# Attention and a gated feed-forward layer on one core: where the row-maximum matmuls stand among the score chunks

## What is computed

```python
def attention(h, ...):                      # h = layernorm(x)
    q, k, v = (proj(W, b) for ...)          # B, 16 heads, 512, 8
    idx = clip(pos[None, :] - pos[:, None], -20, 20) + 20
    attn1 = einsum('bhqd,bhkd->bhqk', q, k)
    attn2 = einsum('bhqd,qkd->bhqk', q, rel_k[idx])
    attn = softmax((attn1 + attn2) / sqrt(8), axis=-1)
    w1 = einsum('bhqk,bhkd->bhqd', attn, v)
    w2 = einsum('bhqk,qkd->bhqd', attn, rel_v[idx])
    return (w1 + w2) @ Wo.T + bo
x = x + attention(layernorm(x))
x = x + ffn(layernorm(x))                   # down(silu(gate) * up)
```

## Time and profile before

| | |
|---|---|
| median of three runs | 1260.71 us (1256.79 to 1262.96) |
| the profiled execution | 1265.17 us, its span 1263.4 us |
| mean granted TensorE clock | 0.991 |
| busy share | TensorE 96%, VectorE 72%, ScalarE 58%, GpSimd 46% |
| attention stage, row maxima | 1024 reductions, 658.5 us of VectorE |
| operand loads and the rest of SyncE's queue | 72.67 MB |

### The profile page before, as it was taken

How to read it: one execution, slowest core, us unless ns; L and a number is a source line. 1 busy time by engine, 2 the same in 40 slices (tenths; PEclk the granted TensorE clock), 3 DMA queues, 4 the chain that set the end, 5 groups by cost and what they waited for, 6 DMA issues and landing times. The chain is left out here.

```text
span 1263.4 us, 60291 instructions
## 1 busy us (share of the span) xinstructions
PE 1207.8 (96%) x27042; PEld 828.2 (66%) x27042; DVE 912.2 (72%) x1747; ACT 735.7 (58%) x1382; POOL 578.1 (46%) x1083
## 2 busy tenths in 40 slices
PE   6988999999999999999999999999999999999998
PEld 4554466767666666666666666676666677666675
DVE  6886877777777767777777777777777776156664
ACT  6885255656666656566666666666666566523322
POOL 5986554444445444443435454444454444022221
PEclk9998999999999989999999999999999999999999
DMA  5776202120203030303021221213030300023221
GB/s 169 228 233 201 54 5 45 34 55 24 63 20 68 12 69 10 70 9 69 22 57 36 52 50 37 57 30 72 20 69 11 70 10 10 12 68 98 77 76 51
DMA packets 101001, 76.52 MB, mean 61 GB/s; under 512 B 12744, under 2 KB 96520, under 8 KB 100744
## 3 DMA queue, kind: packets, MB, share of 16 engines
q1 hardware_dynamic: 100744, 72.67, 22.0%
HBM read 44.86 MB, written 26.21 MB: 56 GB/s over the span
## 5 line engine op out<-in xcount | busy, mean ns | idle before, releaser
L1210 DVE TENSOR_REDUCE b_mx<-b_a 128x1 f32<-128x512 f32 x1024 | 658.5, 685 | 220.5 <-PE b_a L877 218.7
L1155 ACT ACTIVATE b_p<-b_s 128x512 f32<-128x512 f32 x1024 | 569.6, 595 | 366.6 <-PE b_s L936 224.6
L823 POOL TENSOR_TENSOR qd<-q,one 48x512 bf16<-48x512 bf16 x256 | 266.2, 1040 | 453.2 <-PE b_s L936 433.9
L992 PE MATMUL b_pv<-b_p,vg 128*32 128x256 f32 x4096 | 276.3, 383 | 0.0
L936 PE MATMUL b_s<-qd,z 112*128 112x32 bf16 (+1 forms) x6016 | 248.7, 188 | 3.4 <-issue 3.3
L936 PEld LDWEIGHTS b_s<-qd,z 112*128 112x128 bf16 (+1 forms) x6016 | 204.1, 98 | 13.6 <-issue 3.8
L877 PE MATMUL b_a<-k,q 48*128 48x512 bf16 x1024 | 199.8, 386 | 11.3 <-DVE b_mx L1210 3.0
L898 PE MATMUL b_s<-q,k 54*128 54x64 bf16 (+5 forms) x4096 | 186.2, 205 | 8.2 <-DMA q<-b_mt 7.1
L898 PEld LDWEIGHTS b_s<-q,k 54*128 54x128 bf16 (+1 forms) x4096 | 111.4, 95 | 103.0 <-PE b_s L898 29.8
L992 PEld LDWEIGHTS b_pv<-b_p,vg 128*32 128x32 f32 x4096 | 117.4, 109 | 59.8 <-issue 20.3
L945 PE MATMUL b_s<-q,k 118*128 118x64 bf16 x2048 | 104.7, 195 | 2.6 <-issue 2.6
(11 more groups left out here) (146 smaller groups left out, 1263.3 us busy)
## 6 DMA issues: line engine op xcount, KB each, us to landing
x<-in_x SPq DMA_DIRECT2D x24, 256.0 KB, 3.4
scratch_qop<-a_parts SPq DMA_DIRECT2D x16, 384.0 KB, 2.6
scratch_kop<-a_parts SPq DMA_DIRECT2D x16, 384.0 KB, 3.4
k<-scratch_kop SPq DMA_DIRECT2D x32, 192.0 KB
q<-scratch_qop SPq DMA_DIRECT2D x32, 192.0 KB
scratch_v<-a_vr SPq DMA_DIRECT2D x16, 256.0 KB, 3.5
k<-scratch_kop SPq DMA_DIRECT2D x32, 128.0 KB
q<-scratch_qop SPq DMA_DIRECT2D x32, 128.0 KB
```

The costliest lines, as they stand in the source:

```text
L823: nc.gpsimd.tensor_tensor(dst, src, one, ALU.mult).then_inc(s["qd_ready"], 1)
L992: nc.tensor.matmul(PV[V32 * a:V32 * (a + 1), g * PT:(g + 1) * PT], v[:, side, half, t, 2 * a + g, :], PR[pos][:, 4 * a + 2 * half + g, :], ...
L1155: nc.scalar.activation(out, src, ACT.Exp, scale=SCALE).then_inc(s["p_ready"], 1)
L1210: nc.vector.tensor_reduce(MX[unit.v % 2][:, h:h + 1], PA[(HP * n + hp) % NBANK][:, :], AX_X, ALU.max, negate=True).then_inc(s["a_used"], 1)
```

## The change

The diff is given whole. `EXTRA` loses its two entries of pair 1. From pair 1 on `pairs_beside` gives chunks 1 and 9 no row pair and chunks 4 and 12 two; in chunks 2 to 4 and 10 to 12 it counts from one lower, so that the order of row pairs stays unbroken. From pair 1 on they run 16 ahead of the chunks, not 18 as they did from chunk 13 of pair 1 on. The twelve operand loads of an even pair stand one to a chunk in chunks 0 to 11, the value loads in chunk 12.

```diff
-PIECES = ((0, 1), (2,), (3,), (4, 5), (6, 7), (8, 9), (10, 11))
...
-EXTRA = (0, 1, 12, 14, CHUNKS + 4, CHUNKS + 12)
+EXTRA = (0, 1, 12, 14)
...
         n = CHUNKS * pair + c
         first = n + FIRST + sum(e < n for e in EXTRA)
-        return [r for r in range(first, first + 1 + (n in EXTRA)) if r < HH * U]
+        count = 1 + (n in EXTRA)
+        if pair:
+            first -= c in (2, 3, 4, 10, 11, 12)
+            count += (c in (4, 12)) - (c in (1, 9))
+        return [r for r in range(first, first + count) if r < HH * U]
...
                 for c in range(CHUNKS):
-                    if ahead and c < len(PIECES):
+                    if ahead and c < NLOAD:
                         sp.wait_ge(s["s_ready"], PB2 * pair + 2 * c + 1)
-                        load_score_operands(sp, k, d, batch + 1, (batch + 1) % 2, PIECES[c])
-                    if ahead and c == len(PIECES) + 1:
+                        load_score_operands(sp, k, d, batch + 1, (batch + 1) % 2, [c])
+                    if ahead and c == NLOAD:
                         sp.wait_ge(s["s_ready"], PB2 * pair + 2 * c + 1)
                         load_values(sp, k, d, batch + 1, (batch + 1) % 2)
```

## The result

The changed kernel takes 1280.72 us, the median of four runs (1279.23 to 1282.36), against 1261.12 for four runs of the kernel before beside it (1256.79 to 1262.96). The ratio on record is 1.0124, 95% interval 1.0082 to 1.0167. The two medians by themselves give 1.0155; 1.0124 would go with a kernel before of 1265 us, close to its medians in the later sets. So it is slower by 1.2 to 1.6%, clear of noise. Its profiled execution took 1281.19 us, 16.0 more than that of before, with a span of 1278.4, 15.0 more.

What follows compares the result with a forecast made beforehand. TensorE's order and waits were taken to bound the kernel. Terms -26.4 (removed row pairs), +56.0 (doubles), +0.4 (lead) and -14 (loads) gave +16 us, so 1277 us for the median, own range 1268 to 1287, stated range 1266 to 1294.

Steps and rivals of the forecast that it cites:

- The doubles: Second row pairs in chunks 4 and 12, pairs 2 to 30: 0.965 us each, mostly wait, +56.0 us together.
- Rival 4: Second row pair of a double doesn't wait, costing 0.21 us only: 1232 us; chance 0.06.
- The removed row pair: Chunks 1 and 9, pairs 1 to 30: each removal gives 0.44 us of TensorE, -26.4 us together.
- The lead: Row pairs 16 ahead, not 18: +0.4 us for pair 30; minus parts keep about 2.3 us of cover.
- The loads: One load to a chunk in even pairs: -14 us, between 0 and the 21.7 us lost there.
- the guard rows' 8 us: Loads' first term: TensorE's waits for guard rows in even pairs fall, 8 us won, between 6.2 and 9.9.
- The 5 us for "issue" waits: Loads' term for TensorE waits the profile doesn't explain, in loaded pairs, and their clock: 5 us won, bounds 0 and 11.
- The sum: Whole kernel: +16 us on the profiled execution, 1277 us for the median, slower by 1.3%; chance 0.68.
- No relief (1): Waits in the even pairs stay or others take their place: 1260.7 + 30 = 1291 us; chance 0.12.
- Late operands (2): Last q load lands after the next pair's chunk 0 wants it, 1.7 us in 14 pairs: about 1307 us; chance 0.08.
- No clock loss (3): Denies the rival that waits in every pair bring TensorE's clock down: +52 us, 1329 us; chance 0.03.
- That the parts merely cancel (5): Change does less than it says, or some cover is accidental, and parts cancel: near 1261 us; chance 0.03.

Runs made afterwards that it cites:

- one double: Changed kernel with chunk 4 doubled and chunk 1 empty, but one row pair each in chunks 9 and 12: 1267.35 us, ratio 1.0011.
- the one double without idle time, at another place: Changed kernel with second row pairs moved behind value sums in chunk 4 and first value products in chunk 12 (the place meant): 1268.42 us, ratio 1.001.
- the q loads cut: Kernel before with one load to a chunk, lead of 16, q loads of 3 or 2 copies cut into one DMA per copy: 1255.83 us, ratio 0.9918.
- the two experiments that take them apart: Kernel before with only the change's loads and lead: 1256.59 us, ratio 0.993; changed kernel with the old loads: 1295.68 us, ratio 1.0255.
- a better order: Kernel before with spaced loads and lead of 16, q loads before the second half's k loads, value loads in chunk 14: 1250.07 us, ratio 0.9878.

## Why the prediction was right

**The doubles.** Priced at 0.965 each from pair 1, and 0.44 back for each removed row pair: +1.05 per pair. Measured +1.05, and half of it for one double. The price of pair 1 held because nothing in it hung on pair 1: a latency from matmul to maximum to matmul, with VectorE idle ahead of it. Rival 4 (no wait) falls: an emptier chunk 1 before it changed nothing. I expected 60 waits of 0.56 in pairs 1 to 30, two to a pair; the 56 of pairs 2 to 29 are that. My division of the 0.965 into 0.21 of work and 0.75 of wait is not shown: the profile has 0.56 idle, and the one double without idle time, at another place, kept 0.49.

**The removed row pair.** 0.44 forecast; 0.43 in chunk 9. Chunk 1 lasts 1.58 us, not the 1.45 that I named. With its row pair it took 1.90, so 0.32 of the price lay there; the other 0.10 lay at the end of chunk 0, which fell from 1.89 to 662.42 - 660.63 = 1.79.

**The lead.** GpSimd's parts are ready 2.2 us before chunk 2 transposes them; 2.3 was forecast. The first of these rows ends 0.27 later, the second starts the transpose:

```profile
662.29 0.27 POOL L810 TENSOR_TENSOR b_np<-b_r,b_np 128x16 bf16<-128x16 f32 x1
...
664.75 0.24 PE L1045 MATMUL b_mi<-b_idb,b_np 128*32 128x128 bf16 x3
```

I had put the later last load and the later need for operands together at 1 us won, and 1.1 us of waits are gone. Either by itself is far from small: with one row pair to a chunk, the new loads without the shorter lead cost 34.9 us of waits.

**The loads.** -14 forecast, 21.7 - 8.5 = -13.2 measured between the two profiled executions. The kernel with the change's row pairs and the old loads says the same of the loads alone: its pairs 2 to 29 take 865.40 us against the 851.81 of the changed kernel, 13.6 less, and the medians 1295.68 and 1280.72 are 15 apart. But with one row pair to a chunk the same loads win less: 827.21 us against the 834.20 of the lead alone, 7.0, and ratios of 0.993 and 0.9975, whose intervals overlap. The waits for guard rows say why: with the short pairs they only move, from 7.1 us in chunk 6 to 6.1 at the next pair's head, and with the long ones they fall from 10.9 us to 0.4. I had added the loads' gain and the doubles' cost as if neither touched the other; that the full 14 came back hung on the longer pairs, and in that the figure was lucky.

Of its three terms the guard rows' 8 us is borne out (10.9 us of waits with the old loads under the change's row pairs, 0.4 with the new). The 5 us for "issue" waits and their clock is not: they are 4.4 us with the old loads and 3.9 with the new under the same row pairs, and 5.8 with the q loads cut. The clock behind one is seen in pair 4 of the kernel before: TensorE waited 2.0 us and then ran 4.9 us, from 281.1 to 286.0, at a granted clock of 0.50, the lower of its two levels. No run shows what brings these waits about, and each figure is of one execution, so part of the 13.2 may be chance.

**The sum.** +16 forecast, +16.0 between the profiled executions, +19.6 between the medians, which came to 1280.72 where I said 1277. The forecast ratio, 1277 / 1260.71 = 1.0129, lies inside the measured interval. That the median moved more than the profiled execution I put down to spread of the kernel before: its medians of 11 to 25 runs were 1265.5 to 1267.0 later, in other sets. The forecast's own range of 1268 to 1287 doesn't come out of the bounds that I named for it: 0 to -21.7 for the loads and 0.05 on 58 doubles give 1266 to 1294.

**The rivals.** No relief (1) is refuted by the waits view. Its argument that the loads share the queue with the code was misread: the profile lists the code in queues of its own (q8 and q14, 3.51 and 0.35 MB), the loads in q1. Late operands (2) happened once, 0.4 us, at the head of pair 19, and in earnest as soon as the pair was short or the lead long. No clock loss (3): clock 1.00 in each window above, where TensorE waits twice in every pair, so the bank cycling rule of the Trainium skill (TensorE: Matmul & The Clock Gate, A second HAM failure mode) did not bite here. That the parts merely cancel (5) is refuted by the two experiments that take them apart.

## What to carry to other kernels

Before moving a producer's work into pairs, count the buffers between it and its consumer: with three banks and two to a step, a second step can't start before the whole round trip from matmul through reduction to matmul (1.17 us here), even with the consumer idle, and that outweighed the 0.44 us that each removal gave. Ask also what the moved work costs where no wait is left: in chunk 12 it was 0.49 us, so filling the wait would not have saved the idea there. If the kernel already has such a double somewhere, its row in the timeline is the price. Test the parts of a mixed change apart: here the loads and the lead were worth 0.7% as they stood and 1.2% in a better order, and the row pairs took back twice the larger figure.

## What was not expected

The loads and the lead had to move together: spaced loads at the lead of 18 cost 2.55% (two runs), at 16 they gain 0.7%. And a slower kernel can look well fed: the late guard rows cost 6.1 us in 7 pairs of 29.08 us and 0.4 us in one pair of 30.12, with the same loads. A microsecond of slack in each pair hid a fault of the queue's order that, once the pairs were short again, was worth half a per cent (0.993 against 0.9878).
